# Attention: one maximum over the same chunk of both heads, in two pairs of PSUM banks

## The reference, cut to what matters

```
top_u = L // 5                                   # 409
_, top_idx = jax.lax.top_k(query_norms, top_u)
Q_sel = jnp.take_along_axis(Q, top_idx[:, :, None], axis=1)
scores = jnp.einsum('bud,bld->bul', Q_sel, K) * scale
attn = jax.nn.softmax(scores, axis=-1)
out_sel = jnp.einsum('bul,bld->bud', attn, V)
```

## Time and profile before

| | us |
|---|---|
| median of 3 runs | 1077.13 (1076.13 to 1078.85) |
| the profiled execution, its own time | 1078.37 |
| its span, first to last instruction | 1076.2 |
| PE / DVE / ACT / POOL busy | 917.6 / 835.7 / 639.9 / 577.6 |
| granted TensorE clock, mean of the span | 0.925 |

### The profile page before, as it was taken

How to read it: one execution, slowest core, us unless ns; L and a number is a source line. 1 busy time by engine, 2 the same in 40 slices (tenths; PEclk the granted TensorE clock), 3 DMA queues, 4 the chain that set the end, 5 groups by cost and what they waited for, 6 DMA issues and landing times. The chain is left out here.

```text
span 1076.2 us, 26057 instructions
## 1 busy us (share of the span) xinstructions
PE 917.6 (85%) x7437; PEld 593.7 (55%) x7438; DVE 835.7 (78%) x2019; ACT 639.9 (59%) x1443; POOL 577.6 (54%) x581
## 2 busy tenths in 40 slices
PE   5998862699999999997677516999999999999995
PEld 3664442123333333332566415777788888888884
DVE  3677778789999999995767693777787777777773
ACT  3796876378888888886566433455544444444441
POOL 1347761737777777754755402344545545454543
PEclk9999995579999999998799756999999999999998
DMA  7126630521111111401799307998732323232222
GB/s 254 58 95 187 190 99 6 156 78 22 37 22 37 22 37 22 136 6 44 213 255 259 113 1 203 229 235 211 186 55 45 54 39 54 44 49 49 44 45 30
DMA packets 125017, 105.45 MB, mean 98 GB/s; under 512 B 17488, under 2 KB 118544, under 8 KB 124944
## 3 DMA queue, kind: packets, MB, share of 16 engines
q1 hardware_dynamic: 103088, 82.82, 26.1%
q0 software_dynamic: 20480, 20.67, 12.2%
q10 hardware_dynamic: 1376, 1.05, 0.3%
HBM read 50.13 MB, written 31.30 MB: 76 GB/s over the span
## 5 line engine op out<-in xcount | busy, mean ns | idle before, releaser
L1075 DVE TENSOR_REDUCE attend_mxh<-attend_p_a 128x1 f32<-128x512 f32 x416 | 257.1, 677 | 9.8 <-PE attend_p_a L1298 9.1
L1203 ACT ACTIVATE w<-attend_p_b 128x409 f32<-128x409 f32 x512 | 227.6, 516 | 37.4 <-PE attend_p_b L1312 36.1
L2055 ACT ACTIVATE expert_hr<-expert_p,b1t 128x256 f32<-128x256 f32 (+1 forms) x376 | 134.0, 422 | 194.3 <-PE expert_p L1993 172.0
L1948 POOL DMA_INDIRECT out_x<-expert_ys,expert_drop x72 | 127.4, 1769 | 187.7 <-DVE expert_ys L2090 129.0
L2015 PE MATMUL expert_p<-w,expert_hhi 128*128 x800 | 136.7, 273 | 0.7 <-DVE expert_ys L2090 0.3
L1993 PE MATMUL expert_p<-expert_xhi,w 128*128 128x256 f16 x800 | 136.3, 273 | 0.0
L1312 PE MATMUL attend_p_b<-attend_qb,w 64*128 64x409 f16 x512 | 130.8, 345 | 1.5 <-ACT w L1203 1.0
L1298 PE MATMUL attend_p_a<-w,attend_qa 64*128 64x512 f16 x384 | 123.6, 406 | 2.1 <-DVE attend_mxh L1075 1.3
L1338 PE MATMUL attend_p_o<-w,attend_vh 128*32 128x409 f32 x1024 | 116.5, 527 | 1.7 <-issue 0.8
L1938 POOL DMA_INDIRECT expert_xs<-h_d,expert_take x72 | 72.8, 1011 | 76.5 <-issue 63.1
L2015 PE MATMUL expert_p<-w,expert_hlo 128*128 x400 | 109.0, 273 | 0.0
(11 more groups left out here) (378 smaller groups left out, 1802.3 us busy)
## 6 DMA issues: line engine op xcount, KB each, us to landing
expert_wu<-w SPq DMA_DIRECT2D x88, 256.0 KB, 4.1
w<-in_L_ffn_w SPq DMA_DIRECT2D x20, 512.0 KB, 4.0
w<-in_L_attn_x SPq DMA_DIRECT2D x8, 512.0 KB, 11.2
q_d<-q SPq DMA_DIRECT2D x32, 128.0 KB, 1.7
k_d<-w SPq DMA_DIRECT2D x32, 128.0 KB
w<-k_d SPq DMA_DIRECT2D x32, 128.0 KB
attn_d<-zero SPq DMA_DIRECT2D x8, 512.0 KB, 5.7
route_ain<-attn_d SPq DMA_DIRECT2D x32, 128.0 KB, 4.4
```

The costliest lines, as they stand in the source:

```text
L1075: dve.tensor_reduce(mxh[q % 2][:, h, c, k:k + 1], p_a[chunk_use(q, a, h) % CB][:, :], AX, ALU.max).then_inc(a_done, 1)
L1203: act.activation(prob[:, 2 * (j % (TPB // 2)) + h, :], p_b[tile_use(p, j, h) % TB][:, 0:TOP], ACT.Exp, scale=SCALE / UNIT ** 2).then_inc(p ...
L1948: pool.indirect_dma_start(out=out, out_offset=bass.IndirectOffsetOnAxis(ap=drop[u][:, s:s + 1], axis=0), in_=ys[u][:, s, :], in_offset=Non ...
L2055: last = act.activation(hr[g % 2][:, f, rows], p_1[g][:, f, rows], ACT.Relu, bias=cst["b1t"][:, bass.ds(e[s] * FB + 2 * g + f, 1)], scale= ...
```

## The change

The four chunk banks become two tiles of two adjoining banks each. A step a writes head 0's chunk into the first bank and head 1's into the second, and one reduce takes both maxima at once, `[:, :, 512]` to two columns. The semaphores `a_ps` and `a_done` count pairs. PE waits once per step, for the reduce two steps before. Its order inside `scores` becomes tile of head 0, chunk of head 0, chunk of head 1, `between`, tile of head 1. The turn of queries takes a tile bank, at the same place in the order. On DVE `high` follows the negation directly, `low` stands one pair later, `divisors` and `finish` before pairs 7 and 8, the tail's parts before pair 10.

```diff
-        CB, TB = 4, 3
+        CB, TB = 2, 3
-        p_a = [ps(f"p_a{i}", [P, 512], F32) for i in range(CB)]
+        p_a = [ps(f"p_a{i}", [P, 2, 512], F32) for i in range(CB)]
-        USES_A, USES_B = CHP + 1, TIP + 1
         TURN_AT, TAIL_AT = 12, 8
+        TURN_Q, TURN_M = 10, 15
+        USES_B, AT_Q, AT_M = TIP + 2, 2 * TURN_Q, 2 * TURN_M + 1
...
+        def bank_a(q, a):
+
+            return p_a[(NA * q + a) % CB]
+
+        def tile_use(p, j, h):
+
+            return 2 + USES_B * p + 2 * j + h + (j >= TURN_Q) + (j >= TURN_M)
 
         def turn_use(q):
 
-            return 0 if q == 0 else 1 + USES_A * (q - 1) + 2 * TURN_AT
+            return 0 if q == 1 else 2 + USES_B * (q - 2) + AT_Q
...
-                    wait(pool, a_done, min(CHP * (p + 1) + 8 + 2 * at, CHP * NP))
+                    wait(pool, a_done, min(NA * (p + 1) + 4 + at, NA * NP))
...
-                def maximum(q, a, h):
+                def maximum(q, a):
                     c, k = rows_and_keys(a)
-                    dve.wait_ge(a_ps, CHP * q + 2 * a + (1 - h) + 1)
-                    dve.tensor_reduce(mxh[q % 2][:, h, c, k:k + 1], p_a[chunk_use(q, a, h) % CB][:, :], AX, ALU.max).then_inc(a_done, 1)
+                    dve.wait_ge(a_ps, NA * q + a + 1)
+                    dve.tensor_reduce(mxh[q % 2][:, :, c, k], bank_a(q, a)[:, :, :], AX, ALU.max).then_inc(a_done, 1)
...
-                    for s in range(CHP):
-                        if q > 0 and s == 0:
+                    for a in range(NA):
+                        if q > 0 and a == 0:
                             minus_maximum(q - 1)
-                        if q > 0 and s == 1:
                             high(q - 1)
-                        if q > 0 and s == 2:
+                        if q > 0 and a == 1:
                             low(q - 1)
-                        if q > 1 and s == 14:
+                        if q > 1 and a == 7:
                             divisors(q - 2)
-                        if q > 1 and s == 15:
+                        if q > 1 and a == 8:
                             finish(q - 2)
-                        if s == 2 * TAIL_AT + 3:
+                        if a == TAIL_AT + 2:
                             move_tails(q)
-                        maximum(q, s // 2, 1 - s % 2)
+                        maximum(q, a)
...
-                    act.activation(qa[q % 2][:, 0:TOP], p_a[turn_use(q) % CB][:, 0:TOP], ACT.Copy).then_inc(q_done, 1)
+                    act.activation(qa[q % 2][:, 0:TOP], p_b[turn_use(q) % TB][:, 0:TOP], ACT.Copy).then_inc(q_done, 1)
...
-                    wait_chunk_bank(pe, turn_use(q))
-                    turned(q, p_a[turn_use(q) % CB], False).then_inc(q_ps, 1)
+                    wait_tile_bank(pe, turn_use(q))
+                    turned(q, p_b[turn_use(q) % TB], False).then_inc(q_ps, 1)
...
-                def scores_chunk(q, a, h):
+                def chunks(q, a):
...
+                    wait(pe, a_done, NA * q + a - CB + 1)
+                    for h in range(2):
+                        into, rows = bank_a(q, a)[:, h, :], slice(HP * h, HP * h + HP)
...
                 def scores(p, j, ahead=0, a=0, between=None):
 
-                    for h in range(2):
-                        scores_tile(p, j, h)
-                        if ahead and p + ahead < NP:
-                            scores_chunk(p + ahead, a, 1 - h)
-                        if between and not h:
-                            between()
+                    scores_tile(p, j, 0)
+                    if ahead and p + ahead < NP:
+                        chunks(p + ahead, a)
+                    if between:
+                        between()
+                    scores_tile(p, j, 1)
```

More of the change, by code:

```diff
@@ L1085, in minus_maximum @@
                 def minus_maximum(q):
-                    dve.wait_ge(a_done, CHP * (q + 1))
+                    dve.wait_ge(a_done, NA * (q + 1))
                     dve.wait_ge(v_step, VSTEP * q + 1)
@@ L1189, in queries @@
                     act.wait_ge(q_ps, q)
-                    wait(act, a_ps, CHP * (q - 1))
-                    act.activation(qa[q % 2][:, 0:TOP], p_a[turn_use(q) % CB][:, 0:TOP], ACT.Copy).then_inc(q_done, 1)
+                    wait(act, a_ps, NA * (q - 1))
+                    act.activation(qa[q % 2][:, 0:TOP], p_b[turn_use(q) % TB][:, 0:TOP], ACT.Copy).then_inc(q_done, 1)
                 def queries_max(p):
```

58 lines of the change are left out of this document (19 added, 39 removed).

## The result

The changed kernel takes 1080.43 us (median of 19 runs, 1077.49 to 1089.42) beside 1078.08 us for the kernel before (19 runs, 1075.80 to 1080.87). The ratio is 1.0029, 95% interval 1.0016 to 1.0041: slower by 1.7 to 4.4 us, where half a microsecond less was forecast. One run of all the experiments, of a_finish, took 1523.62 us in a slower state and is left out of its ratio. The profiled execution of the changed kernel took 1085.47 us, 5 us over its own median; why it is that far above is a part of the answer.

The account below looks back on a forecast made before the run. DVE led PE by half a microsecond, POOL's 18.15 us round setting the average; afterwards PE bounds: 16.8+0.15+0.36+0.2 = 17.5, taken as 17.45. Overall -0.4-0.7+0.5+0.1 = -0.5: 1077.9 us profiled, 1076.6 median, range 1071.8 to 1084.6.

Parts of the forecast that it names:

- Reduces: DVE's maxima: 13 reduces of 1024 at 1.12 us replace 26 of 512 (1.19 for two), 0.9 us less per round.
- wait of pair 10: Pair 10's chunks wait for pair 8's reduce, which comes behind DVE's results: +0.15 us a round, bounds 0 and +0.64.
- The order on PE: Three times a round a product splits a group of tiles and chunks: +0.18 before it, -0.06 behind, together +0.36 us.
- DVE's wait and the turn of queries: PE's 0.5 us wait for DVE per head pair disappears; the turn's use of tile banks costs +0.2, bounds 0 and 0.5.
- Bank pairs and `finish`: PE at most two bank pairs ahead of DVE's reduces: only +0.15 us a round, at pair 10; no cost for moving `finish`.
- Against POOL: POOL's L994 keeps holding DVE's `high`, rounds near 18.1 us: -0.7 us for slipping, +0.5 for `high` standing nearer the negation.
- The floor: POOL's L989 ahead of the last pair's turn of queries: no more than 4.0 plus 0.4 us can be gained.
- The clock: PE's granted clock, read as 1.00 in the window of one head pair; no term for falls in the rounds.
- PE in strict order: Rival, chance 0.20: chunk 1 cannot start before chunk 0, groups end 0.18 us later, rounds of 18.2, +6.5 us, 1083.6.
- Too shallow pairs: Rival, chance 0.11: waits at both tight bank-pair places reach their bound and recur, rounds of 17.9, no hold, 1079.4 us.
- The second rival's sum: Rival, chance 0.30: POOL's hold on DVE's `high` breaks, seven rounds run at 17.45 us; terms summed to -3.9, 1073.2.

Follow-up runs that it names:

- a_finish: Changed kernel with `finish` directly behind `divisors`, ahead of pair 7's reduce: 1078.32 us, ratio 0.9999 against the kernel before.
- b_order: Kernel before with only PE's new order (tile 0, chunk 0, chunk 1, `between`, tile 1), single banks and 26 reduces kept: 1082.56 us, ratio 1.0043.
- b_late_finish: Kernel before with `finish` taken one reduce later on DVE: 1079.77 us, ratio 1.0020.
- b_turn: Kernel before with only the turn of queries moved to the tile banks: 1077.69 us, ratio 0.9995.
- a_dummy: Changed kernel with pair 9's chunks computed one extra time, without a signal, ahead of the round's first product: 1076.26 us, ratio 0.9996.
- b_spread_early: Kernel before with POOL's tensor operation for V (`spread_v`, L994) moved ahead of its gathers: 1076.65 us, ratio 0.9990.
- b_turn_spread2: Kernel before with the turn of queries in the tile banks and POOL's `spread_v` ahead of its gathers: 1077.05 us, ratio 0.9993.
- a_fill: Changed kernel with pair 9's chunks moved ahead of the round's first product and not issued again: 1080.25 us, ratio 1.0022.
- a_old_order: Changed kernel with PE's old order inside a group (tile 0, chunk 1, tile 1, chunk 0): 1090.6 us, ratio 1.0121.
- a_finish_dummy_spread: Changed kernel with `finish` behind `divisors`, extra unsignalled chunks ahead of the first product, and POOL's `spread_v` ahead of the gathers: 1095.18 us, ratio 1.0158.
- b_late_dummy2: Kernel before with `finish` one reduce later and one chunk of step 9 computed an extra time ahead of the first product: 1078.68 us, ratio 1.0001.
- b_high_scalar: Kernel before with `high` made by a multiplication with a constant, one tensor input instead of two: 1078.14 us, ratio 1.0008.

## Why the prediction was wrong

Two terms were put at nothing: the move of `finish` (+0.36 us from the results to the first product of a round, and with it an idle gap of 0.33 to 0.45 us on PE) and the granted clock, taken as a constant 1.00 (four falls in each profile, 1.5 us each). The second makes the sign of the result; the first opens the gap at which the falls begin. Every other term of the round is right to 0.2 us, the sum in part by luck.

*Reduces: right.* 208 records of 1.22 us, a step of 1.13 between two that follow each other (3.49 us for three, less the 1.22 of the last, over two) against 1.12 taken.

*The round, place by place.* From product to product, the changed kernel less the kernel before, in rounds of 17.72 and 17.26:

| stretch | before | after | forecast | measured |
|---|---|---|---|---|
| results to first product | 3.04 | 3.40 | 0 | +0.36 |
| the three groups that a product splits | 1.59, 1.54, 1.53 | 1.70, 1.72, 1.71 | 3 x 0.18 | +0.47 |
| the stretches behind them (the results' own included) | 1.32, 1.32, 1.54 | 1.27, 1.27, 1.53 | 3 x -0.06 | -0.11 |
| products to the two turns | 1.34, 1.35 | 1.40, 1.40 | 0 | +0.11 |
| turn of queries to its next product | 1.42 | 1.05 | -0.5 + 0.2 | -0.37 |
| wait of pair 10 | | none | +0.15 | 0 |

The sum is +0.46 where the forecast had +0.21 (and rounded it to less).

*The order on PE: right but for 0.2* (+0.47 and -0.11 against +0.36, and 0.11 ahead of the turns). b_order warns that this is so with the pairs only: with single banks the order costs 0.8.

*DVE's wait and the turn of queries: right in sum, wrong in its parts.* The 0.5 us of true wait for DVE lie in the stretch behind the turn. b_late_finish has 1.03 us there with four single banks and the turn in its old place: it is enough that PE was held up earlier in the round. So the -0.37 need not be a gain of the pairs, and the +0.36 may in part be this wait in another place. I took -0.5 for the pairs and +0.2 for the tile bank. b_turn has the second alone and it is a gain, 1.42 to 1.14: with one use less in the ring of chunk banks, the chunk that waited no longer does, or less (argued, not traced). My bounds of 0 and 0.5 excluded a gain without a reason.

*Bank pairs and `finish`: the first step that failed.* I walked the 13 pairs against their banks and found 0.15 at pair 10, where no idle time of PE shows in the changed kernel. I did not walk `finish`. The text of the change says where it stands, and I costed that move at nothing: the stretch from 276.04 to 278.12 was "ACT's". That was so, but DVE's results ended only 0.10 us ahead of the product, and the next delay of them had to show. One pair reduce instead of one single reduce between `divisors` and `finish` is +0.54 on DVE (1.09 less 0.55) and +0.36 from the results to the first product, where the forecast had 0, and 0.15 (bounds 0 and 0.64) at pair 10 for all of DVE's work around there. The difference, 0.21, is nearly all of what the sum of the round, +0.21, lacks to the +0.46 measured. (The working gave 17.51 for the round and took 17.45 without a reason.) a_finish shows that the order of `finish` alone does not set it: moved, the same time is lost one product later.

*Against POOL.* At 17.78 DVE drifts towards POOL by 0.4 us a round instead of the 0.7 forecast, and with the four falls on top it never arrives within fourteen (without them, in a_dummy and a_finish, it does for the last two or three); `high` stays at 0.20:

```profile
L1089 DVE TENSOR_TENSOR attend_qrow<-attend_mneg,attend_steps 128x8 f16<-128x8 f32 x6 | 1.2, 198 | 0.6
```

(six of them in 355 to 464 us, where before they took 1.26 each). So the slower round is nearly paid for by the missing hold, 14 x 17.78 = 248.9 against 247.97. None of my cases had this one. The floor was right (b_spread_early, b_turn_spread2).

*The clock: the second step that failed, missing altogether.* Without the falls the change has -0.8 ahead of the rounds and +0.9 in them: nothing, where -0.5 was forecast. a_dummy, the changed kernel without falls in its rounds, is there: ratio 0.9996, 1076.3 us, close to the 1076.6 of the forecast, by other terms and so by luck. What lifts the measured median to 1080.4 is, by the profiles, the falls, 1.5 us each, about three a run if all of it is theirs (an estimate from the 4.2 us between the two medians); that all of it is theirs is not shown, since a_fill is slow without them. The profile of before had the granted clock at 1.00 through all its rounds, to 491 us, and I took it for a constant. Its gaps ahead of the first product were 0.25 us at most.

*PE in strict order: refuted.* It would give the sign that was measured, for another reason. In the changed kernel's timeline the first chunk (276.91) starts with the tile of 276.90, and the next ones 0.2 us behind: in the trace's single records the chunk that raises the pair's semaphore, issued last, on the free half, is the one at 276.907, and head 0's chunk, issued before it, starts at 277.084. The Trainium skill's rule of strict order ("TensorE: Matmul & The Clock Gate", The mechanism) does not hold here between halves of the array. It has a second side: the signalling chunk ends at 277.293 and head 0's chunk at 277.460 (modelled ends), so the signal alone does not say that both banks are written. In the whole stage the nearest reduce starts 0.045 us behind the modelled end of head 0's chunk. Who takes this change over should let both chunks signal.

*Too shallow pairs:* the time of 1079.4 was near, the mechanism not; by the list of waits PE never stands idle for a reduce in 240 to 480 us of the changed kernel. Weight loads of chunks wait up to 0.4 us for one, the tail's pair most, behind tiles that run meanwhile, as the walk had it.

*The second rival's sum* does not come out: its terms, -4.5, +0.8 for the passing touches, +0.8 and -0.4, give -3.3 and 1073.8, not -3.9 and 1073.2. The verdict does not hang on it.

## What to carry to other kernels

Walk every reader of a bank against the next writer, the small ones too: here three tiny result operations on DVE, between two of the big reduces, decided when PE's next product could start, and a move "one step later" doubled in length with the step. Where PE's work is thin, a new gap of 0.3 to 0.7 us may cost not its own length but 1.5 us each time that the granted clock falls at it; look at the clock row by windows, over more than one profile, and test by filling the gap with work that nobody needs. And a fill has waits of its own: check which buffer it writes before it is combined with another repair.

## What the runs showed of the hardware that I had not expected

- At idle gaps of 0.33 to 0.85 us, once a round in a stage where PE is otherwise busy, the granted clock fell from 1.00 to 0.50 for 3.4 us. It comes in some rounds and not in others that look alike (four of fifteen in two profiles of the changed kernel, in different places; three in b_late_finish, seven in a_old_order, eight in a_finish_dummy_spread), and not at all in 240 to 480 us of b_order, which has no such gap, nor of a_dummy. It does not come either in b_late_dummy2, whose gaps are 0.36 to 0.63, nor at the gaps of 1.3 us in b_turn_spread2: the gap's length is not the whole condition, and what else is stays open.
- One or two extra matmuls of 0.39 us a round ahead of that product, none of them used, kept the clock at 1.00 from 240 to 480 us.
- Of two matmuls on different halves of the array, the one issued later can start first, here by 0.18 us.
- DVE's `high` of 8 elements a partition is held for 1.27 us by POOL's operation of 1.28 with two tensor inputs and with one alike.
- That hold works as a phase lock: in the kernel before, b_turn and b_high_scalar the whole chain of PE, DVE and ACT goes at POOL's 18.15 us a round, and the list of waits names nobody for it.
